# First layer of a two-layer attention kernel: float32 scores from row-tiled queries and keys instead of a stack of bf16 parts

## What is computed

```python
# first layer, window attention: windows of 8x8 = 64 tokens, 16 heads of 16 channels, image rolled by 4
q, k, v = (xw @ Wq.T), (xw @ Wk.T), (xw @ Wv.T + bv)      # per window and head
qn = q / max(norm(q), 1e-12);  kn = k / max(norm(k), 1e-12)
logits = einsum('bhnd,bhmd->bhnm', qn, kn) * exp(min(logit_scale, log 100))
logits = logits + 16 * sigmoid(bias)                        # bias of a small network, one table per head
logits = where(shift_mask, -inf, logits)                    # 4 regions of the rolled image
o = softmax(logits) @ v;   z = o @ Wo.T + bo
x = x + first_layer(group_norm(x))
# second layer: attention over the 256 tokens of an image, 8 heads look back and 8 ahead, no bias
x = x + second_layer(group_norm(x))
```

## Time and profile before

| | us |
|---|---|
| median of 3 runs | 1645.87 |
| lowest, highest | 1627.16, 1653.5 |
| the profiled execution | 1622.35 |
| its span, first to last instruction | 1620.6 |
| mean granted TensorE clock over the span | 0.899 of full speed |

### The profile page before, as it was taken

One profiled execution on the slowest core, in us unless ns is written; L12 is line 12 of the kernel. 1 busy time (PEld: TensorE's weight loads), 2 busy tenths in 40 slices (PEclk: granted clock), 3 DMA queues, 4 the chain that ended last, 5 costly groups with the idle time before them and its releaser, 6 DMA issues. The chain is left out here.

```text
span 1620.6 us, 42349 instructions
## 1 busy us (share of the span) xinstructions
PE 1353.1 (83%) x16602; PEld 967.5 (60%) x16602; DVE 944.0 (58%) x1704; ACT 643.5 (40%) x1101; POOL 421.6 (26%) x397
## 2 busy tenths in 40 slices
PE   6458778767787867777757999999999999999997
PEld 3235555555565545455545677777777777777764
DVE  1558778867767767876434445555455554555541
ACT  2324434433344333344211444444444444444442
POOL 0114434332343333334320121112111211112111
PEclk9578889877888878787868999999999999999998
DMA  4567687779777768866710011111111121111112
GB/s 87 97 90 125 95 124 119 117 95 129 111 110 105 106 105 113 121 105 81 113 26 11 8 34 37 34 29 39 39 36 32 29 39 39 36 32 29 39 40 59
DMA packets 277146, 114.11 MB, mean 70 GB/s; under 512 B 144334, under 2 KB 267984, under 8 KB 276944
## 3 DMA queue, kind: packets, MB, share of 16 engines
q1 hardware_dynamic: 273980, 112.70, 44.0%
q10 hardware_dynamic: 3104, 0.53, 0.2%
HBM read 70.72 MB, written 41.94 MB: 70 GB/s over the span
## 5 line engine op out<-in xcount | busy, mean ns | idle before, releaser
L1122 DVE TENSOR_REDUCE cm<-psG 128x4 f32<-128x1024 f32 (+1 forms) x256 | 245.3, 958 | 314.5 <-PE psG L952 314.4
L1071 ACT ACTIVATE probs<-psG 128x1024 f32<-128x1024 f32 (+1 forms) x256 | 207.7, 811 | 228.8 <-PE psG L928 228.8
L1174 POOL TENSOR_SCALAR_AFFINE_SELECT probs<-probs 128x1024 f32<-128x1024 f32 x128 | 139.7, 1091 | 607.6 <-ACT probs L1071 607.6
L692 POOL TENSOR_TENSOR probs<-probs,ebias 128x1024 f32<-128x1024 f32 x64 | 150.6, 2354 | 398.5 <-ACT probs L503 398.5
L916 PE MATMUL psG<-stack 32*128 32x512 f32 (+1 forms) x1024 | 234.7, 534 | 7.9 <-ACT probs L1071 7.8
L943 PE MATMUL psG<-stack 32*128 32x256 f32 (+1 forms) x2048 | 236.7, 348 | 5.3 <-DVE cm L1122 4.1
L368 PE MATMUL psA<-probs,xh 128*128 128x512 f32 x256 | 156.8, 744 | 19.2 <-DVE rest L657 13.4
L943 PEld LDWEIGHTS psG<-stack 32*128 32x128 f32 x2048 | 155.4, 185 | 13.0 <-DVE cm L1122 5.2
L635 DVE TENSOR_REDUCE cm<-psG 128x8 f32<-128x512 f32 x128 | 82.2, 685 | 96.4 <-PE psG L392 96.2
L405 PE MATMUL psG<-stack 101*64 101x64 bf16 x2048 | 50.8, 209 | 100.7 <-DMA stack<-ct 99.5
L503 ACT ACTIVATE probs<-psG 128x1024 f32<-128x1024 f32 x64 | 65.5, 1023 | 171.3 <-PE psG L405 170.6
(11 more groups left out here) (111 smaller groups left out, 2208.0 us busy)
## 6 DMA issues: line engine op xcount, KB each, us to landing
stack<-scratch_parts SPq DMA_DIRECT2D x384, 128.0 KB, 6.4
scratch_parts<-parts SPq DMA_DIRECT2D x32, 768.0 KB, 3.4
X<-in_xr SPq DMA_DIRECT2D x32, 256.0 KB, 3.3
scratch_heads<-on SPq DMA_DIRECT2D x64, 128.0 KB, 3.0
rows<-scratch_heads SPq DMA_DIRECT2D x32, 256.0 KB, 3.0
out<-X SPq DMA_DIRECT2D x32, 256.0 KB, 2.2
probs<-in_wop SPq DMA_DIRECT2D x1, 1024.0 KB
probs<-in_wqk SPq DMA_DIRECT2D x1, 512.0 KB
```

The lines of the kernel that those rows point to most:

```text
L692: nc.gpsimd.tensor_tensor(both, both, ebias[:, :, :], ALU.mult).then_inc(biased, 1)
L1071: nc.scalar.activation(weights[:, at:at + 4 * b.size].rearrange("p (r x) -> p r x", r=2), banks, ACT.Exp).then_inc(exp_done, 1)
L1122: nc.vector.reduce_max(cm[o][:, b.queries_of, :].rearrange("p (r x) -> p r x", x=COL)[:, first:first + 2, 0:2], banks.rearrange("p r (e k) ...
L1174: nc.gpsimd.affine_select(out=diagonal, in_=diagonal, compare_op=ALU.is_ge, fill=0.0, base=0, pattern=[[0, 8], [sign, P]], channel_multipl ...
```

## The change

The stack, the parts, their transfers and the bounds' transfer are gone. `copy_qk` copies the turned queries to `qt` and the turned keys twice to `km`, each copy with one of two neighbouring heads' rows zeroed (`own` is a 0/1 column per partition). A row tile of 32 rows then holds two heads. `bounds` and `scores` multiply float32 queries and keys on four row tiles (`own_rows(r)`, bank r of `G`) and two column tiles (`e * WTOK`). Region masks and bounds are added by bf16 matmuls of the same tile shape (`region_queries`, `region_keys`, `pick`, `ct`). All of PSUM's four G banks serve in turn for the scores and the bounds, so `bounds(i+1)` waits for both exponentials of image i. The maxima are taken in two instructions of 1024 columns.

The values `vw` lie by window and head, 32 columns wide with zeros beside 16 of them. The row sums are 32 matmuls of 64 columns with the selector `sel` into 64 columns of `E`; DVE takes the reciprocal of 64 columns (`invert_sums`), POOL spreads it over 512 (`spread_blocks`), TensorE over the partitions (`spread_sums`), ACT copies the weighed values to SBUF (`copy_o`), and `outputs` multiplies. `output` needs 8 matmuls of 128 columns in place of 16. Several `tensor_tensor` and one `tensor_scalar` of DVE become `scalar_tensor_tensor`. The bias table is laid out by row tile and built with 16 short activations; a `prepare` on PE and DVE makes the selectors.

```diff
+            def scores(i):
+                wait(pe, c_out, i.count(1))
+                wait(pe, exp_done, i.plus(-1).count(2))
+                if i.plus(3).among(images):
+                    wait(pe, gn_chain, i.plus(3).count(3, 1))
+                for o in range(CT):
+                    for w in range(WINDOWS):
+                        for e in range(2):
+                            for r in range(QUADS):
+                                at = r * 512 + o * TOKENS + w * WTOK
+                                nc.tensor.matmul(G[e * WTOK:(e + 1) * WTOK, at:at + WTOK], km[i.k][own_rows(r), o, w, e, :],
+                                                 qt[i.k][own_rows(r), o, win(w)], start=(o == 0 and w == 0), stop=False,
+                                                 tile_position=(r * COL, e * WTOK), skip_group_check=True)
+                for o in range(CT):
+                    for e in range(2):
+                        for r in range(QUADS):
+                            at = r * 512 + o * TOKENS
+                            last = nc.tensor.matmul(G[e * WTOK:(e + 1) * WTOK, at:at + TOKENS], pick[own_rows(r), 2 * o + e, :],
+                                                    ct[own_rows(r), :], start=False, stop=True, ...)
+            def bounds(i):
+                wait(pe, qk_out, i.count(QK_OPS))
+                wait(pe, exp_done, i.plus(-1).count(2))
...
+                                nc.tensor.matmul(G[ww * WTOK:(ww + 1) * WTOK, at:at + P], qt[i.k][own_rows(r), o, win(2 * t + ww)],
+                                                 km[i.k][own_rows(r), o, 2 * t + ww, :, :], start=(t == 0 and o == 0), stop=False,
+                                                 tile_position=(r * COL, ww * WTOK), skip_group_check=True)
...
+            def project_v(i):
+                wait(pe, o_out, i.plus(-2).count(1))
+                for w in range(WINDOWS):
+                    for c in range(CT):
+                        for e in range(2):
+                            last = nc.tensor.matmul(A[2][e * WTOK:(e + 1) * WTOK, w * P:(w + 1) * P], xh[i.k][:, c, win(w)],
...
+            def turn(i):
+                wait(pe, qkn_done, i.count(2))
...
+            def sums(i):
+                wait(pe, biased, i.count(2))
+                wait(pe, z_out, i.plus(-1).count(2))
+                for n in range(8):
+                    for r in range(QUADS):
+                        last = nc.tensor.matmul(E[own_rows(r), 0:WTOK], sel[:, n, :], prob[i.k][:, r, n // WINDOWS, n % WINDOWS, :],
...
+            def spread_sums(i):
+                wait(pe, rdx_done, i.count(1))
+                nc.tensor.matmul(E[:, :], spread, rdx, start=True, stop=True).then_inc(spread_done, 1)
...
+            def copy_qk(i):
+                wait(act, turned, i.count(2, 1))
+                wait(act, s_ready, i.plus(-2).count(QUADS))
+                nc.scalar.activation(qt[i.k][:, :, :].rearrange("p o t -> p (o t)"), A[0][:, :], ACT.Copy).then_inc(qk_out, 1)
+                wait(act, turned, i.count(2))
+                for e in range(2):
+                    nc.scalar.activation(km[i.k][:, :, :, e, :].rearrange("p o w k -> p (o w) k"),
+                                         A[1][:, :].rearrange("p (n k) -> p n k", k=WTOK), ACT.Copy,
+                                         scale=own[:, e:e + 1]).then_inc(qk_out, 1)
...
             def outputs(i):
-                wait(dve, sums_done, i.count(QUADS))
-                wait(dve, o_done, i.plus(-1).count(1))
-                nc.vector.reciprocal(rd[:, :], B[1]).then_inc(r_done, 1)
...
+                wait(dve, spread_done, i.count(1))
+                wait(dve, o_out, i.count(1))
+                raw = ot[:, :, :].rearrange("p o t -> p (o t)")
+                nc.vector.tensor_tensor(raw, E[:, :], raw, ALU.mult).then_inc(o_done, 1)
...
-                    nc.vector.tensor_tensor(rs_t[:, :], rs_t[:, :], rs[:, :], ALU.mult).then_inc(newton, 1)
+                    nc.vector.scalar_tensor_tensor(out=rs_t[:, :], in0=rs_t[:, :], scalar=1.0, in1=rs[:, :],
+                                                   op0=ALU.mult, op1=ALU.mult).then_inc(newton, 1)
...
+            def add_bias(i, part):
+                wait(pool, exp_done, i.count(2, part + 1))
...
+                nc.gpsimd.tensor_tensor(both, both, bias.unsqueeze(2).to_broadcast([P, 4, WINDOWS, WTOK]),
+                                        ALU.mult).then_inc(biased, 1)
+            def spread_blocks(i):
+                wait(pool, r_done, i.count(1))
+                wait(pool, spread_done, i.plus(-1).count(1))
+                nc.gpsimd.tensor_tensor(rdx.rearrange("p (n q) -> p n q", q=WTOK), rd[:, :].unsqueeze(1).to_broadcast([P, 8, WTOK]),
+                                        block_of[:, :].unsqueeze(2).to_broadcast([P, 8, WTOK]), ALU.mult).then_inc(rdx_done, 1)
```

More of the change, by code:

```diff
@@ new lines, in output @@
+            def output(i):
+                wait(pe, o_done, i.count(1))
+                for o in range(CT):
+                    dst = E[:, o * TOKENS:(o + 1) * TOKENS].rearrange("p (t rr ww c) -> p t ww rr c", t=TT, rr=WIN, ww=2)
+                    for t in range(TT):
+                        for f in range(CT):
+                            last = nc.tensor.matmul(dst[:, t], wo[:, f, o * P:(o + 1) * P],
+                                                    ot[:, f, t * P:(t + 1) * P].rearrange("p (ww rr c) -> p ww rr c", ww=2, rr=WIN),
+                                                    start=(f == 0), stop=(f == CT - 1))
+                last.then_inc(z_ready, 1)
@@ L360, in weigh @@
-                last.then_inc(pv_done, 1)
+                    wait(pe, v_out, i.plus(1).count(2))
+                for o in range(CT):
+                    for w in range(WINDOWS):
+                        for r in range(QUADS):
+                            at = o * TOKENS + w * WTOK
+                            last = nc.tensor.matmul(A[2][own_rows(r), at:at + WTOK], vw[i.k][:, w, QUADS * o + r, :],
+                                                    prob[i.k][:, r, o, w, :], start=True, stop=True,
+                                                    tile_position=(0, r * COL), skip_group_check=True)
+                            if o == CT - 1 and w == WINDOWS - 1:
+                                last.then_inc(pv_done, 1)
@@ L370, in project, with turn_c @@
                 last.then_inc(proj_qk, 1)
-            def project_v(i):
-                wait(pe, c_out, i.plus(-1).count(1))
+            def turn_c(i):
+                wait(pe, max_done, i.count(2))
                 for t in range(TT):
-                    for c in range(CT):
-                        last = nc.tensor.matmul(A[2][:, t * CH:(t + 1) * CH], xh[i.k][:, c, t * P:(t + 1) * P],
-                                                wv[:, c, :], start=(c == 0), stop=(c == CT - 1))
-                last.then_inc(proj_v, 1)
@@ L398, in scores @@
-            def scores(i, t):
-                wait(pe, c_row[i.k], i.dmas(1))
-                wait(pe, exp_done, i.count(2, t - 1 + 1) if t else i.plus(-1).count(2))
-                rows = slice(0, STACK + MASKS + 1)
-                for h in range(HEADS):
-                    for ww in range(2):
-                        last = nc.tensor.matmul(C[0][WTOK * ww:WTOK * (ww + 1), h * WTOK:(h + 1) * WTOK],
-                                                stack[i.k][rows, 1, h, win(t, ww)], stack[i.k][rows, 0, h, win(t, ww)],
-                                                start=True, stop=True, skip_group_check=True)
-                last.then_inc(s_ready, 1)
@@ L500, in exponent @@
[L500 to L503 removed]
+                    rows = slice(half * WTOK, (half + 1) * WTOK)
+                    for r in range(QUADS):
+                        nc.scalar.activation(ebias[rows, r, :, half * HALF:(half + 1) * HALF], by_parity[rows, half, r],
+                                             ACT.Exp, scale=16.0).then_inc(a_tab2, 1)
+                        nc.scalar.activation(across[rows, r, :, :], by_parity[rows, 1 - half, r], ACT.Exp,
+                                             scale=16.0).then_inc(a_tab2, 1)
```

414 lines of the change are left out of this document (196 added, 218 removed).

## The result

| | before | after |
|---|---|---|
| median of 4 runs, us | 1649.68 | 1540.86 |
| lowest, highest | 1627.16, 1666.74 | 1536.2, 1546.19 |
| the profiled execution, its span | 1622.35, 1620.6 | 1546.19, 1544.5 |
| mean granted clock over the span | 0.899 | 0.927 |

The ratio is 0.9417, 95% interval 0.931 to 0.9523: 5.8% faster. The forecast was 1465 with a range of 1390 to 1615. The sign and the range held; the forecast's own narrower range, 1430 to 1500, did not.

A forecast was written before the change was run, and what follows sets the result against it. TensorE was taken to set the step: 16.8 us of work plus a 2.45 us hole ahead of `turn`, 19.25 us. Layer 0's 689 us plus layer 1's 773.6 made 1463, 1464 with surroundings, given as 1465, range 1390 to 1615.

The forecast's parts named there:

- DVE's chain: Ahead of `turn`: statistics, seeds, nine Newton steps and `unit_qk`, done at 6.8 us without POOL, 11.35 with it.
- the sum: Layer 0 at 689 us plus layer 1 at 773.6: 1463 us of span, 1464 with the 1.75 around it.
- step 0: Start of the first layer's steps: at 80 us against 97.3 before, with `turn(0)` staying at 54.55.
- steps 0 to 28: First layer: 29 steps of 19.25 us each, 558 us, from 16.8 of TensorE work and a 2.45 hole.
- step 29: First layer, the step without projection: 15.7 us.
- steps 30 and 31 and the end: First layer's close: 13.4 us for each step, then 8 us for the last output, residual and statistics.
- Small matmuls: In `scores` and `bounds`: 22 ns a record, making the stages 3.3 and 1.9 us.
- my lower bound of 13.7: Nearest case below for `scores`: 13.7 ns a record on four column tiles, 2.0 us for 144 records.
- the floor of the weights: For small matmuls on row tiles: a floor from the 128-column weights, 22 ns for 64 columns.
- Where POOL catches DVE: Ahead of `turn`: POOL runs 4.55 to 9.25 us, holding the seventh and eighth Newton steps; `turn` starts at 11.35.
- POOL blocks on: Rival, chance 0.2: the residual also holds DVE, hole 3.5 us or more, half clock, step 23.8 us, total 1600.
- The hole and the clock: Ahead of `turn`: a hole of 2.45 us, below the earlier 3.11 and 3.32, so full clock (2.4 GHz).

The follow-up runs named there:

- e7: The kernel before without its 14 transfers per image, the stack's scores left out of the computation; 1568.4 us, 0.9589 of before.
- e4: The changed kernel with DVE's four `scalar_tensor_tensor` forms turned back into `tensor_tensor` and `tensor_scalar`; 1531.38 us, 0.9357 of before.
- e6: The changed kernel with the loop over the four row tiles outermost in `scores` and `bounds`, so consecutive matmuls share a row tile; 1545.05 us, 0.9436 of before.
- e5: The changed kernel with five extra float32 matmuls of 512 columns, results unread, on TensorE between `bounds` and `turn`; 1535.39 us, 0.9376 of before.
- e2: The changed kernel, but POOL's first bias multiplication of an image waits until that step's Newton steps are done; 1447.92 us, 0.8845 of before.
- e11b: The kernel of e2 with TensorE's list of stages rotated so its hardware loop closes between `turn` and `sums`; 1447.23 us, 0.8821 of before.
- e3: The kernel of e2 with both halves of `project` placed between `turn` and `sums` on TensorE; 1482.89 us, 0.9065 of before.

## Why the prediction was right, and where it was off

**Right in kind.** The transfers' waits went (e7: 4.1%), DVE's chain took their place ahead of `turn` (as forecast), the new instruction forms bought nothing (e4), layer 1 is unchanged: 1544.5 - 770.26 = 774.2 us against 773.6.

**The sum, term by term.** The profiled execution is 1546.19 - 1464 = 82 us above the sum. It is made of: step 0 at 86.12 where 80 was forecast (6.1); steps 0 to 28, 29 of them, from 86.12 to 720.68, 21.88 in the mean for 19.25 (76.3); step 29, without a projection, 17.4 for 15.7 (1.7); steps 30 and 31 and the end, 32.2 from 738.05 to 770.26 for 26.8 + 8 (-2.6); layer 1 (0.6). The steps with a projection are the miss. (The 22.9 us that I read for a step of before averages in a short last one: its steps 0 to 28 take 23.6 in the mean. No term of the sum used it.)

**Small matmuls: 22 ns forecast, 10.7 measured.** (1.54 - 0.22) / 123 for the scores, (1.19 - 0.27) / 62 = 15 ns for the bounds. That is below my lower bound of 13.7, which came from four tiles; these are eight. The two stages take 1.75 and 1.42 us, 3.2 together where I had 5.2, and the floor of the weights that I read out of the earlier trace rows does not show. The Trainium skill's floor of about 25 ns from start to start (TensorE: Matmul & The Clock Gate, section "Wait — 56ns, not 53.3ns?") is contradicted by it for matmuls on tiles; 25 ns is what e6 shows when neighbours share a row tile. TensorE reached `turn` 7.04 us into the step (420.96 - 413.92), not 8.9.

**Where POOL catches DVE.** The forecast had POOL start at 4.55, six Newton instructions done and one left to go behind POOL's second part, `turn` at 11.35. The scores were 1.55 us shorter, so POOL started at 3.01, before the first Newton instruction; eight are left at 7.67, which take 2.7 us, scale and shift 0.3, `unit_qk` 1.34: `turn` at 12.16. The early start is not what cost the 0.8 us. Two DVE instructions pass, one for each part of `add_bias`, and each costs about 2.1 us, whichever they are: in e6 POOL starts at 4.89, holds the last two Newton instructions and leaves none behind, and `turn` comes at 12.08. The sentence of the prediction that an earlier POOL catches an earlier instruction and hardly moves `turn` was right. The 0.8 us are mainly two other terms. The seeds began 2.54 us into the step (416.46) where the forecast had 2.15, 0.28 of it a wait between `norms` and the seeds. And, as the rival "POOL blocks on" allowed, the residual held DVE too, but little: 0.71, 0.31 and 0.31 us for 0.23, that is 0.6 us in all.

**The hole and the clock: the step that failed.** Turn 0.8 us later and TensorE 1.9 us earlier make the hole 5.12 us for 2.45, and in the next step 5.5. Behind it came 1.2 GHz, where the forecast had full clock: `turn` to the next `scores` took 10.41 us (426.08 to 436.49) for 7.87, 2.5 us. With the 0.8 this is the whole 3.3 us by which the step of 22.57 exceeds 19.25; in the next one `turn` is 1.2 us late and the clock costs 1.35. I had taken full clock because holes of up to 3.11 us had left it full and one of 3.32 had not the earlier trace rows, and 2.45 is below both. That comparison doesn't hold: e6 had a hole of 1.82 us and lost the same 2.5 us behind it. So cheap small matmuls made the hole long, but a shorter hole did not keep the clock; where TensorE worked through the hole, in the undisturbed steps of e5, it stayed full (1.00, 7.88 us from `turn` to the scores). Why 1.82 us was enough in e6 and 3.11 not enough before stays open. The rival "POOL blocks on" had this mechanism, the residual holding on and half clock, with 23.8 us for a step; the truth lies at 22.2 in the mean of two steady steps, nearer to it than to the 19.25. I gave it 0.2, which was too little, and its condition for the clock, a hole of 3.5 us or more, was too strict. That the time still fell inside the stated range is owed to that range, which was drawn wide enough to hold the rival, and not to the forecast's own step.

**A wait I had not named.** The scores' first weight load waits 0.76 us for DVE's `variances`, the third condition in the diff. It costs next to nothing: `spread_sums` to `scores` is 1.04 us, for 0.9 forecast.

**The start.** The first `turn` comes at 64.33, 9.8 us later than before, not up to 3: TensorE waits 15.49 us for `unit_qk` there, 10.23 before. The chain ahead of it shows where about half of it arose, ACT in order of time:

```profile
56.67 1.38 ACTq L499 DMA_DIRECT2D ebias<-probs  x2
58.10 0.60 ACT L505 ACTIVATE probs<-psA 128x512 f32<-128x512 f32 x1 [1.46 <-issue]
```

The reciprocal of the table starts at 49.80 (45.45 before); where those 4.4 us come from was not followed up. And `finish_table` with its 16 activations (53.24 to 56.64) and these two transfers now stands on ACT ahead of `square(1)` of the first image (L505), for which DVE waits 5.64 us; before, DVE took the norms straight behind the reciprocal. I had put that work beside the path, and it was on it; no kernel was run to try another order. From there to step 0 it was 21.8 us, for 25.5 forecast.

## What to carry to other kernels

When long GpSimd instructions with both operands in SBUF start while VectorE is in a chain of short ones that TensorE waits for, add to the chain the length of one GpSimd instruction for each of them: each let one VectorE instruction pass here, and it made no difference which (`turn` at 12.08 us with the last two held, 12.16 with the first two). An explicit wait that lets VectorE's chain finish first was worth 6% here (e2 against the change), though GpSimd starts later. A faster stage ahead of such a meeting gives nothing to the step; it only lengthens the hole (e6). And when a forecast leaves a hole in TensorE's work at every step, give half the clock behind it a chance of its own, even if a longer hole elsewhere left the clock full: in e6 1.82 us was enough.

## What the runs showed of the hardware that was not expected

- Float32 matmul records of 32 rows and 64 columns on eight tiles (four row, two column) start 10.7 ns apart; in an order in which neighbours share a row tile, 25 ns.
- Two back-to-back GpSimd products of 2.35 us each let one VectorE instruction through apiece. A VectorE instruction with one tensor input (L651, a `tensor_scalar`, 2.37 us for 0.20) is held like those with two. The Trainium skill (SBUF — State Buffer, section "SBUF: two separate sides") has the exclusive lock, and the rows agree with it; that one instruction gets through between two GpSimd instructions is what they add.
- The half clock doesn't follow from a hole's length alone. In e6 holes of 1.82 and 2.40 us come in turn and both are followed by 1.2 GHz, the shorter one by more of it: the granted clock is 0.73 from 416.9 to 427.3 and 0.84 from 440.0 to 449.2. In e11b a hole of 2.57 us was followed by 1.2 GHz and one of 2.43 by full clock, in neighbouring steps; before, 3.11 us left it full. The two steps of e11b, the sums (L416) with the hole ahead of them, and `project` (L442), eight records in 4.43 and in 3.70 us:

```profile
410.88 1.17 PE L416 MATMUL psE<-probs 128*32 128x64 f32 x64 [2.57 <-POOL probs L740]
...
413.69 4.43 PE L442 MATMUL psA<-probs,xh 128*128 128x512 f32 x8
...
430.63 1.10 PE L416 MATMUL psE<-probs 128*32 128x64 f32 x64 [2.43 <-POOL probs L740]
...
432.56 3.70 PE L442 MATMUL psA<-probs,xh 128*128 128x512 f32 x8
```

- TensorE stood up to 3.2 us at a time around the end of its hardware loop, with nothing that releases it in the profile, 63.5 us in all between 100 and 650 us in e3 and 4.5 in e11b, whose body is as long. The order of the stages decided where this fell and how much of it was hidden.
